# A two-layer graph attention kernel: every transfer of 125 rows issued as 112 rows and 13 rows

## The chip, the cores and the metric

The kernel runs on one core of one Trainium2 chip. The metric is the device time in microseconds of one execution. Before the change the median of three runs is 1033.21 us (1032.12 to 1034.33).

## The reference

Two graph attention layers over 1250 nodes and 20000 edges (plus a self loop for every node), then a residual sum and a layer norm. The first layer has 4 heads of 512 channels, the second one head of 768.

```python
def _gat_layer(x, src, dst, W, a_src, a_dst, bias, concat):
    h = (x @ W).reshape(N, H, C)
    al_s = jnp.einsum('nhc,hc->nh', h, a_src)
    al_d = jnp.einsum('nhc,hc->nh', h, a_dst)
    e = jax.nn.leaky_relu(al_s[src] + al_d[dst], 0.2)
    m = jax.ops.segment_max(e, dst, num_segments=N)
    ex = jnp.exp(e - m[dst])
    denom = jax.ops.segment_sum(ex, dst, num_segments=N)
    alpha = ex / (denom[dst] + 1e-16)
    out = jax.ops.segment_sum(h[src] * alpha[:, :, None], dst, num_segments=N)
    out = out.reshape(N, H * C) if concat else out.mean(axis=1)
    return out + bias

h = jax.nn.elu(_gat_layer(x, ..., W1, att_src1, att_dst1, b1, concat=True))   # 1250 x 2048
out = _gat_layer(h, ..., W2, att_src2, att_dst2, b2, concat=False)            # 1250 x 768
result = layernorm(x + out)
```

## The kernel before

The 1250 nodes are cut into 10 blocks of 125 (`B`), and 125 is the partition count of nearly every tile. The edges become a dense matrix of counts, `C[dst, src]`, and attention is done densely on it: per block of 125 destinations a row of 1250 scores, its exponential, times the counts, transposed on TensorE (line 476), and multiplied with the features `h`. Every product in float32 is made of three matmuls of split operands (lines 1243 to 1245, the helper `products`), so a block of a head costs 30 matmuls of 512 columns.

The stages in order of time:

- 0 to about 205 us: the edge lists become counts, x is loaded (`xall`, lines 486 to 489), transposed and stored (`xT_scratch`, L501), head 0's `h` is made.
- 205 to 684 us: four heads. Per block `j` of a head: TensorE makes the product, VectorE turns it into `vbuf` (L1099), ScalarE makes `ebuf` in two steps (L820, L822), VectorE finishes it (L1114), and SyncE stores 125 x 512 floats of `ebuf` into the DRAM scratch `hidden_scratch` (L535, `store_hid`). `ebuf` has two slots, so ScalarE at block j first waits until the store of block j-2 has landed (`hid_stored`, in `step` of the scalar program). Between two heads TensorE makes the next head's `h` from `xr` (L531, 128 rows), which is loaded back in blocks of 750 KB into three slots.
- 684 to about 872 us: the second layer's `h2`. Each block of 125 hidden rows of 2048 floats is loaded back (`hblk`, L545, `load_hb`, two slots), transposed on TensorE (L1353) and multiplied with `W2p`, which is 16 chunks `c` of 128 rows. Chunks 0 to 5 are loaded before the last head (`w2raw`) and split into high and low parts by ScalarE (L802) and GpSimd (L634) during its blocks 6 to 8. Chunks 6 to 15 (`w2late`, L538) are loaded after the last store of the last head; ScalarE (L802) and VectorE (L1129) split them.
- about 872 to 1030 us: second attention, with `xres` (L591) and `b2row` (L586) for residual and bias, and the store of `out` (L595) per block. The program ends when SyncE has seen all stores of `out` land.

All transfers are issued by SyncE, in program order, on one queue. What the order is at the turn from the heads to the second layer, in SyncE's program: at block 6 of the last head, the loads of `hblk` for blocks 0 and 1, then the stores of `ebuf` of blocks 6, 7, 8 and 9, then the ten loads of `w2late`, then two loads of `a2row`, then the other loads of `hblk`. An instruction that waits on SyncE holds all that stand behind it.

The transfers of 125 rows are: `b1row` (1000 KB, a broadcast), the 40 stores to `hidden_scratch` (250 KB each), the 10 loads of `hblk` (1000 KB each), two of `a2row` and one of `b2row` (375 KB, broadcasts), 10 loads of `xres` and 10 stores of `out` (375 KB each): 74 in all. The load of `xall` was already in two parts, rows 0 to 111 and rows 112 to 124 (`XP`). All others have 128 or 80 rows.

Of the kernel before, what the change touches and what calls it, by code (L numbers as in the profile page):

```python
# [26 lines left out]
B = 125  # L27
NB = N // B
PAIRS = E // (2 * B)
D = 768  # L30
# [33 lines left out]
WRING = 3  # L64
XL = 2
XP = 112
XW = 2
XR = 3

# [27 lines left out]
def gat_kernel(nc, x, src, dst, W1, as1, ad1, b1, W2, as2, ad2, b2, out):  # L97
# [4 lines left out]
    with ExitStack() as ctx:  # L102
# [378 lines left out]
        @block.sync  # L481
        def _(sp):
            sp.dma_start(dst_i[:], dst.rearrange("(p u e) -> p u e", u=2, e=B)).then_inc(ld_dst, 16)
            sp.dma_start(src_i[:], src.rearrange("(p u e) -> p u e", u=2, e=B)).then_inc(ld_src, 16)

            for i in range(NB // XL):
                for lo, hi in ((0, XP), (XP, B)):
                    sp.dma_start(xall[lo:hi, XL * i:XL * (i + 1), :], x[XL * i * B:XL * (i + 1) * B, :]
                                 .rearrange("(b p) d -> p b d", p=B)[lo:hi, :, :]).then_inc(ld_x[i], 16)

            def load_w1(h):
                sp.dma_start(w1raw[:], W1[:, h * HC:(h + 1) * HC].rearrange("(k p) c -> p k c", p=128)
                             ).then_inc(ld_w1, 16)

            sp.wait_ge(xt_ps, NB)
            load_w1(0)

            for j in range(NB):
                sp.wait_ge(xt_lo, j + 1)
                for u in range(2):  # L500
                    sp.dma_start(xT_d[j, :, u, :].rearrange("p (k n) -> p k n", k=KD), xa[:, u, :, j, :].bitcast(F32)).then_inc(xT_stored, 16)  # L501
            sp.wait_ge(ranges, 1)
            sp.dma_start(attr[:, 0:H, :], as1.rearrange("(o h) c -> o h c", o=1).broadcast_to([128, H, HC])
                         ).then_inc(ld_att, 16)
            sp.dma_start(attr[:, H:2 * H, :], ad1.rearrange("(o h) c -> o h c", o=1).broadcast_to([128, H, HC])
                         ).then_inc(ld_att, 16)

            sp.wait_ge(xT_stored, 32 * NB)  # L510
            sp.wait_ge(w1_hi, KD)
            sp.wait_ge(w1_lo, KD)
            for n in range(2 * KD):
                if n >= 3:
                    sp.wait_ge(wa_done, H * (n - 2))
                sp.dma_start(w1raw[:, 2 * (n % 3):2 * (n % 3) + 2, :],
                             W1[128 * (n // 2):128 * (n // 2) + 128, bass.ts(n % 2, 2 * HC)]
                             .rearrange("p (a c) -> p a c", a=2)).then_inc(ld_wk[n % 3], 16)
            sp.wait_ge(wa_done, 2 * H * KD)
            load_w1(1)  # L520


            sp.wait_ge(rows_ps, 3)
            sp.wait_ge(mm_done, NB)
            sp.dma_start(b1row[:], b1.rearrange("(o n) -> o n", o=1).broadcast_to([B, HID])).then_inc(ld_b1, 16)

            def load_xr(h, j):
                u = NB * (h - 1) + j
                if u >= XR:
                    sp.wait_ge(mm_done, 2 * NB * ((u - XR) // NB + 1) + (u - XR) % NB + 1)  # L530
                sp.dma_start(xr[:, u % XR, :, :].bitcast(F32), xT_d[j]).then_inc(ld_xr[u % XR], 16)  # L531

            def store_hid(h, j, s):
                sp.wait_ge(hid_done, NB * h + j + 1)
                sp.dma_start(hid_d[bass.ds(j * B, B), h * HC:(h + 1) * HC], ebuf[:, s, :]).then_inc(hid_stored[s], 16)  # L535

            def load_w2(c):
                sp.dma_start(w2_raw(c), W2[128 * c:128 * c + 128, :]).then_inc(ld_w2[c], 16)  # L538

            def load_hb(b, s):  # L540
                if isinstance(b, int) and b < 2:
                    sp.wait_ge(hid_stored[s], 8 * (H - 1) * NB + 16)
                else:
                    sp.wait_ge(ht_ps, 2 * b - 2)
                sp.dma_start(hblk[:, s, :], hid_d[bass.ds(b * B, B), :]).then_inc(ld_hb[s], 16)  # L545

            for h in range(H):
                if h == H - 1:
                    sp.wait_ge(mm_done, 2 * NB * (H - 1) + NB)
                    for c in range(WR):  # L550
                        load_w2(c)
                if h + 1 < H:
                    for j in range(XR):
                        load_xr(h + 1, j)

                def head(j, s):

                    if h == H - 1 and isinstance(j, int) and j == NB - 4:
                        load_hb(0, 0)
                        load_hb(1, 1)  # L560
                    store_hid(h, j, s)
                steps(sp, NB, 0, 4, head)
                if h + 1 < H:
                    for j in range(XR, NB):
                        load_xr(h + 1, j)
                if h + 2 < H:
                    sp.wait_ge(w1_hi, KD * (h + 2))
                    sp.wait_ge(w1_lo, KD * (h + 2))
                    load_w1(h + 2)


            sp.wait_ge(mm_done, 2 * H * NB)
            sp.wait_ge(v_done, H * NB)
            sp.wait_ge(w2_lo_p, WR)
            for c in range(WR, KC):
                if c >= KC - 2:
                    sp.wait_ge(hid_stored[c % 2], 16 * H * NB // 2)
                load_w2(c)
            sp.dma_start(a2row[:, 0, :], as2.broadcast_to([B, D])).then_inc(ld_a2, 16)
            sp.dma_start(a2row[:, 1, :], ad2.broadcast_to([B, D])).then_inc(ld_a2, 16)  # L580
            with sp.Fori(1, NB // 2) as k:
                for u in range(2):
                    load_hb(2 * k + u, u)

            sp.wait_ge(al2_done, 2 * NB)
            sp.dma_start(b2row[:], b2.rearrange("(o n) -> o n", o=1).broadcast_to([B, D])).then_inc(ld_b2, 16)  # L586

            def load_xres(b, s):
                if not (isinstance(b, int) and b < 2):
                    sp.wait_ge(y_b, b - 1)  # L590
                sp.dma_start(xres[:, s, :], x[bass.ds(b * B, B), :]).then_inc(ld_xres[s], 16)  # L591

            def store_out(b, s):
                sp.wait_ge(y_done, b + 1)
                sp.dma_start(out[bass.ds(b * B, B), :], y[:, bass.ds(b, 1), :].rearrange("p o n -> p (o n)")  # L595
                             ).then_inc(out_stored, 16)

            load_xres(0, 0)
            load_xres(1, 1)
            with sp.Fori(1, NB // 2) as k:  # L600
                for u in range(2):
                    load_xres(2 * k + u, u)
                    store_out(2 * k + u - 2, u)
            store_out(NB - 2, 0)
            store_out(NB - 1, 1)
            sp.wait_ge(out_stored, 16 * NB)


        @block.gpsimd
        def _(pool):  # L610
# [51 lines left out]
                pool_add(pool, H * NB + j, j % 2, prow2, arow2[:])  # L662

            def add_bias(b, s):
                pool.wait_ge(ld_xres[s], 8 * (b - s) + 16)
                pool.tensor_tensor(xres[:, s, :], xres[:, s, :], b2row[:], ALU.add).then_inc(xb_done, 1)

            pool.wait_ge(ld_b2, 16)
            add_bias(0, 0)

            def step2(j, s):
# [9 lines left out]
        def _(act):  # L681
# [122 lines left out]
            for h in range(H):  # L804
# [29 lines left out]
                        scores(nxt(4)[0], nxt(4)[1], s)  # L834

                def stored(h, j, s):
                    return 16 * (NB // 2) * h + 8 * (j - s)

                def split_w1_of(h1, k):
                    if isinstance(k, int) and k == 0:  # L840
# [19 lines left out]
            for c in range(W2E, KC):  # L860
                split_w2(c)
            for i in range(2):
                act.wait_ge(hid_stored[i], 16 * H * NB // 2)

            def h2_step(b, s):
                split_hT(2 * b + 2, b + 1, 0)
# [57 lines left out]
        def _(dve):  # L924
# [155 lines left out]
            dve_counts(dve, 2, 2, 0, prow)  # L1080
            dve_split(dve, 1, 1, PThi, PTlo)
            dve.wait_ge(bc_sb, H)
            dve.wait_ge(ld_b1, 16)

            def split_hT(n, half):
                dve.wait_ge(ht_hi, n + 1)
# [40 lines left out]
            for c in range(W2E, KC):  # L1127
                dve.wait_ge(w2_hi, c + 1)
                dve.tensor_tensor(W2p[:, c, 1, :], w2_raw(c), W2p[:, c, 0, :].bitcast(F32), ALU.subtract  # L1129
                                  ).then_inc(w2_lo, 1)  # L1130
            dve.wait_ge(ld_a2, 32)

            def scores2(b, s):

# [35 lines left out]
            maxima2(3)  # L1170
            dve_counts(dve, G2 + 2, 2, 0, prow2)
            dve_split(dve, G2 + 1, 1, PT2hi, PT2lo)
            dve.wait_ge(ld_b2, 16)

            def step2(j, s):
                g = G2 + j
# [14 lines left out]
                    dve_counts(dve, g + 3, j + 3, 1 - s, prow2)  # L1191
                if more(2):
                    dve_split(dve, g + 2, s, PT2hi, PT2lo)
                dve.wait_ge(ld_b2, 16)
                dve.wait_ge(y_b, j + 1)
                for a in range(2):
                    last = dve.bn_stats(bnst[:, a, :], y1[:, a * DH:(a + 1) * DH])
                last.then_inc(y_st, 1)
                dve.wait_ge(ld_b2, 16)
                dve.wait_ge(y_st, j + 1)  # L1200
                dve.bn_aggr(mv[:],
                            bnst[:].rearrange("p a n -> p (a n)")).then_inc(y_mv, 1)
# [11 lines left out]
        def _(pe):  # L1214
# [131 lines left out]

            def transpose_h(b, s, half):
                if half == 0:
                    pe.wait_ge(ld_hb[s], 8 * (b - s) + 16)
                if not (isinstance(b, int) and b == 0):  # L1350
                    pe.wait_ge(ht_lo, 2 * b + half - 1)
                for k in range(KH):
                    t = pe.transpose(PS[:, ht_banks(half)[k // 4], (k % 4) * B:(k % 4 + 1) * B],  # L1353
                                     hblk[:, s, (half * KH + k) * 128:(half * KH + k + 1) * 128], ident[0:B, 0:B])
                t.then_inc(ht_ps, 1)
# [124 lines left out]
```

## Time and profile before

| | |
|---|---|
| median of 3 runs | 1033.21 us |
| the profiled execution's own time | 1031.99 us |
| its span in the profile | 1030.2 us |
| TensorE (PE) busy | 913.7 us, 89% |
| VectorE (DVE) busy | 619.3 us, 60% |
| ScalarE (ACT) busy | 401.3 us, 39% |
| GpSimd (POOL) busy | 210.1 us, 20% |
| the 16 DMA engines, mean share | 29.1% |

The span is cut into 40 slices on the page. TensorE is at 9 tenths or more in nearly all slices from 220 to 870 us. Its dips after that are at about 875 to 900 us; a short one lies at 684 to 690 us, and the last 10 us have no matmul. "DMA share" in a window is the mean busy share of the core's 16 DMA engines, so one engine at work all the time counts 0.0625. In a timeline row the two numbers in front are the start and the duration in microseconds; for SPq rows that merge several issues, the duration reaches from the first to the end of the last. A bracket names how long the engine was idle before, and what it waited for.

### The profile page before, as it was taken

What the parts mean: (1) busy time and instruction counts of PE and PEld (TensorE: products, weight loads), DVE (VectorE), ACT (ScalarE), POOL (GpSimd) and SP (SyncE); (2) the same over time, 40 slices, a digit from 0 to 9 for tenths busy, and PEclk for the clock granted to TensorE, in tenths of its full rate; (3) what the DMA queues carried; (4) which work ended last, traced back from release to release, by engine and by line L of the source; (5) the groups of instructions that cost most, each with busy time, mean ns of one, the idle gap of its engine ahead of it and who ended that gap; (6) DMA issues with size and microseconds to landing.
All of it is one profiled execution on the core that took longest, in us unless ns stands there. A gap on an engine that the chain in (4) does not pass through costs nothing.

```text
span 1030.2 us, 13905 instructions
## 1 busy us (share of the span) xinstructions
PE 913.7 (89%) x4740; PEld 786.4 (76%) x4740; DVE 619.3 (60%) x1305; ACT 401.3 (39%) x574; POOL 210.1 (20%) x113
## 2 busy tenths in 40 slices
PE   0676788979999999999999999979999998479996
PEld 0454566668787788878887788869999998479995
DVE  9666568379987456863578645443221222988874
ACT  6454531256651366514663155542111112622220
POOL 1002000225530145202442023410000000343432
PEclk9987999989999999999999999989999999689998
DMA  6009975040115410263003431252111100101122
GB/s 155 1 7 191 150 227 171 7 128 27 32 32 191 179 31 29 66 219 126 30 30 102 138 103 37 93 191 111 58 63 40 74 6 1 44 21 57 59 64 69
DMA packets 38710, 86.65 MB, mean 84 GB/s; under 512 B 17251, under 2 KB 17411, under 8 KB 37032
## 3 DMA queue, kind: packets, MB, share of 16 engines
q1 hardware_dynamic: 38663, 86.04, 29.1%
q8 instruction: 28, 0.46, 0.2%
q14 instruction: 19, 0.16, 0.1%
HBM read 64.27 MB, written 21.76 MB: 84 GB/s over the span
## 4 chain that ended last, share of the span: by engine, by line
issue 38%; PE 27%; DVE 10%; ACT 8%; POOL 8%; SPq 4%; DMA 4%; DVEq 0%; POOLq 0%; ACTq 0%
PE ps L1243 7%; PE ps L1245 7%; PE ps L1244 7%; POOL prow L419 5%; SPq L501 4%; DVE junk_w L1032 2%; POOL W1lo L629 2%; PE ps L1353 2%; DMA hidden_scratch<-ebuf 2%; DMA xT_scratch<-xa 1%; PE ps L1274 1%; ACT prow L414 1%; DVE nbr L437 1%; DVE prow L456 1%; ACT oh_lo L701 1%
## 5 line engine op out<-in xcount | busy, mean ns | idle before, releaser
L419 POOL TENSOR_TENSOR prow<-prow,arow 125x1250 f32<-125x1250 f32 x50 | 139.3, 2789 | 633.4 <-ACT prow L414 633.4
L1243 PE MATMUL ps<-hhi,PThi 125*125 125x512 f32 x400 | 162.2, 405 | 1.0 <-DVE hlo L1019 1.0
L1244 PE MATMUL ps<-hlo,PThi 125*125 125x512 f32 x400 | 158.5, 396 | 0.0
L1245 PE MATMUL ps<-hhi,PTlo 125*125 125x512 f32 x400 | 158.1, 395 | 0.0
L425 ACT ACTIVATE prow<-prow,expb 125x1250 f32<-125x1250 f32 x50 | 67.0, 1340 | 172.7 <-POOL prow L419 151.5
L1243 PE MATMUL ps<-W2p,hT 128*125 128x384 f32 x320 | 110.6, 346 | 6.7 <-DVE W2p L1129 5.6
L1245 PE MATMUL ps<-W2p,hT 128*125 128x384 f32 x320 | 108.7, 340 | 0.0
L1244 PE MATMUL ps<-W2p,hT 128*125 128x384 f32 x320 | 108.5, 339 | 0.0
L1088 DVE TENSOR_TENSOR hT<-ps,hT 128x500 fp32r<-128x500 f32 x40 | 25.3, 674 | 128.4 <-ACT hT L797 124.0
L476 PE MATMUL ps<-ident,prow 125*125 125x125 f32 x500 | 68.1, 286 | 28.4 <-DVE prow L456 12.2
L476 PEld LDWEIGHTS ps<-ident,prow 125*125 125x125 f32 x500 | 65.0, 199 | 35.0 <-issue 30.6
L456 DVE SCALAR_TENSOR_TENSOR prow<-prow,counts 125x1250 f32<-125x1250 f32 x50 | 74.4, 1488 | 26.1 <-ACT prow L425 25.3
L1245 PEld LDWEIGHTS ps<-hhi,PTlo 125*125 125x125 f32 x400 | 74.6, 187 | 19.4
L1243 PEld LDWEIGHTS ps<-hhi,PThi 125*125 125x125 f32 x400 | 74.7, 187 | 18.6 <-DVE hlo L1019 1.5
L1244 PEld LDWEIGHTS ps<-hlo,PThi 125*125 125x125 f32 x400 | 74.6, 186 | 17.0
L441 DVE CUSTOM_DVE_ANT_0 nbr<-nbr,arow 125x1250 bf16<-125x1250 bf16 x50 | 77.3, 1546 | 2.1
L1046 DVE TENSOR_SCALAR ring<-table,ekey 125x420 bf16<-125x420 uint16 (+1 forms) x210 | 56.0, 341 | 34.5 <-issue 11.7
L694 ACT ACTIVATE hhi<-ps 125x512 fp32r<-125x512 f32 (+1 forms) x40 | 23.8, 597 | 134.9 <-PE ps L1245 134.9
L1243 PE MATMUL ps<-W1hi,xr 128*125 128x512 f32 x180 | 71.2, 396 | 2.1 <-DMA xr<-xT_scratch 2.1
L797 ACT ACTIVATE hT<-ps 128x500 fp32r<-128x500 f32 x40 | 21.3, 584 | 132.2 <-PE ps L1353 132.2
L1099 DVE SCALAR_TENSOR_TENSOR vbuf<-ps,rden,b1row 125x512 f32<-125x512 f32 x40 | 29.8, 746 | 69.1 <-PE ps L1245 69.1
L1244 PE MATMUL ps<-W1lo,xr 128*125 128x512 f32 x180 | 71.1, 395 | 0.0
(157 smaller groups left out, 1818.2 us busy)
## 6 DMA issues: line engine op xcount, KB each, us to landing
xr<-xT_scratch SPq DMA_DIRECT2D x30, 750.0 KB, 4.4
hidden_scratch<-ebuf SPq DMA_DIRECT2D x40, 250.0 KB
hblk<-hidden_scratch SPq DMA_DIRECT2D x10, 1000.0 KB
xT_scratch<-xa SPq DMA_DIRECT2D x20, 375.0 KB, 13.2
w1raw<-in_L_gnn_W SPq DMA_DIRECT2D x4, 1536.0 KB, 7.7
w1raw<-in_L_gnn_W SPq DMA_DIRECT2D x12, 512.0 KB, 3.6
w2late<-in_L_gnn_W SPq DMA_DIRECT2D x10, 384.0 KB, 8.0
xres<-in_x SPq DMA_DIRECT2D x10, 375.0 KB
```

The lines of the kernel that those rows point to most:

```text
L419: pool.tensor_tensor(buf[:, s, :], buf[:, s, :], row, ALU.add).then_inc(e_done, 1)
L425: act.activation(buf[:, s, :], buf[:, s, :], ACT.Exp, scale=SLOPE, bias=expb[:, bass.ds(g, 1)]).then_inc(p_done, 1)
L441: dve.tensor_tensor_reduce(out=scr[:], in0=scr[:], in1=row, scale=1.0, scalar=-3.0e38, op0=ALU.add, op1=ALU.max, accum_out=mx[:]).then_inc ...
L456: dve.scalar_tensor_tensor(buf[:, s, :], buf[:, s, :], 1.0, C[:, bass.ds(b, 1), :].rearrange("p o n -> p (o n)"), ALU.min, ALU.mult, accum ...
L476: t = pe.transpose(PS[0:B, 2 + bank, (b - lo) * B:(b - lo + 1) * B], buf[:, s, b * B:(b + 1) * B], ident[0:B, 0:B])
L501: sp.dma_start(xT_d[j, :, u, :].rearrange("p (k n) -> p k n", k=KD), xa[:, u, :, j, :].bitcast(F32)).then_inc(xT_stored, 16)
L1046: oh = dve.tensor_scalar(ring[:, w % 2, v, 0:win_cols(w)], table[:, w % TR, 0:win_cols(w)], ekey[:, bass.ds(at_slot(first, i, v), 1)], Non ...
L1088: lo = dve.tensor_tensor(ht_part(half, 1, a), PS[:, bank, 0:4 * B], ht_part(half, 0, a).bitcast(F32), ALU.subtract)
L1099: dve.scalar_tensor_tensor(vbuf[:, s, :], PS[0:B, s, :], rden[:, bass.ds(g, 1)], b1row[:, h * HC:(h + 1) * HC], ALU.mult, ALU.add).then_in ...
L1243: pe.matmul(dst, ahi, bhi, start=start, stop=False)
L1244: pe.matmul(dst, ahi, blo, start=False, stop=False)
L1245: return pe.matmul(dst, alo, bhi, start=False, stop=stop)
```

## The change

Each of the 74 transfers becomes two: rows 0 to 111 and rows 112 to 124 of the same tile, with the matching rows in DRAM. Both parts add 16 to the same semaphore, so every wait on one of these semaphores is doubled (`RS` is 32). Nothing else differs: buffers, engines, order and all other transfers are as before.

```diff
+RP = ((0, XP), (XP, B))
+RS = 16 * len(RP)
...
-            sp.dma_start(b1row[:], b1.rearrange("(o n) -> o n", o=1).broadcast_to([B, HID])).then_inc(ld_b1, 16)
+            for lo, hi in RP:
+                sp.dma_start(b1row[lo:hi, :], b1.rearrange("(o n) -> o n", o=1).broadcast_to([hi - lo, HID])).then_inc(ld_b1, 16)
...
             def store_hid(h, j, s):
                 sp.wait_ge(hid_done, NB * h + j + 1)
-                sp.dma_start(hid_d[bass.ds(j * B, B), h * HC:(h + 1) * HC], ebuf[:, s, :]).then_inc(hid_stored[s], 16)
+                for lo, hi in RP:
+                    sp.dma_start(hid_d[bass.ds(j * B + lo, hi - lo), h * HC:(h + 1) * HC], ebuf[lo:hi, s, :]).then_inc(hid_stored[s], 16)
...
                 if isinstance(b, int) and b < 2:
-                    sp.wait_ge(hid_stored[s], 8 * (H - 1) * NB + 16)
+                    sp.wait_ge(hid_stored[s], RS // 2 * (H - 1) * NB + RS)
                 else:
                     sp.wait_ge(ht_ps, 2 * b - 2)
-                sp.dma_start(hblk[:, s, :], hid_d[bass.ds(b * B, B), :]).then_inc(ld_hb[s], 16)
+                for lo, hi in RP:
+                    sp.dma_start(hblk[lo:hi, s, :], hid_d[bass.ds(b * B + lo, hi - lo), :]).then_inc(ld_hb[s], 16)
...
-            sp.dma_start(a2row[:, 0, :], as2.broadcast_to([B, D])).then_inc(ld_a2, 16)
-            sp.dma_start(a2row[:, 1, :], ad2.broadcast_to([B, D])).then_inc(ld_a2, 16)
+            for lo, hi in RP:
+                sp.dma_start(a2row[lo:hi, 0, :], as2.broadcast_to([hi - lo, D])).then_inc(ld_a2, 16)
+                sp.dma_start(a2row[lo:hi, 1, :], ad2.broadcast_to([hi - lo, D])).then_inc(ld_a2, 16)
...
             def store_out(b, s):
                 sp.wait_ge(y_done, b + 1)
-                sp.dma_start(out[bass.ds(b * B, B), :], y[:, bass.ds(b, 1), :].rearrange("p o n -> p (o n)")
-                             ).then_inc(out_stored, 16)
+                for lo, hi in RP:
+                    sp.dma_start(out[bass.ds(b * B + lo, hi - lo), :], y[lo:hi, bass.ds(b, 1), :].rearrange("p o n -> p (o n)")
+                                 ).then_inc(out_stored, 16)
...
-            sp.wait_ge(out_stored, 16 * NB)
+            sp.wait_ge(out_stored, RS * NB)
...
                 def stored(h, j, s):
-                    return 16 * (NB // 2) * h + 8 * (j - s)
+                    return RS * (NB // 2) * h + RS // 2 * (j - s)
```

`b2row` and `xres` are changed in the same way, and the waits for `ld_b1`, `ld_a2`, `ld_b2`, `ld_xres`, `ld_hb` and `hid_stored` on the other engines likewise. The programs of TensorE, VectorE, ScalarE and GpSimd keep every instruction and its place; only SyncE gets rows.

SyncE before, from the loads of `hblk` for blocks 0 and 1 in the last head to the first loop of the second layer:

```order
L545 DMA hblk<-hidden_scratch 125x2048 x2
L535 DMA hidden_scratch<-ebuf 125x512 x4
L538 DMA w2late<-in_L_gnn_W 128x768 x10
L579 DMA a2row<-in_L_gnn_att_src 125x768
L580 DMA a2row<-in_L_gnn_att_dst 125x768
```

SyncE now, at the same place:

```order
L550 DMA hblk<-hidden_scratch 112x2048
L550 DMA hblk<-hidden_scratch 13x2048
L550 DMA hblk<-hidden_scratch 112x2048
L550 DMA hblk<-hidden_scratch 13x2048
L539 DMA hidden_scratch<-ebuf 112x512
L539 DMA hidden_scratch<-ebuf 13x512
L539 DMA hidden_scratch<-ebuf 112x512
L539 DMA hidden_scratch<-ebuf 13x512
L539 DMA hidden_scratch<-ebuf 112x512
L539 DMA hidden_scratch<-ebuf 13x512
L539 DMA hidden_scratch<-ebuf 112x512
L539 DMA hidden_scratch<-ebuf 13x512
```

Behind these twelve the ten loads of `w2late` stand as before. Between the last product's store and the first load of `w2late` there is one more issue than before, and the load of `a2row` is now four issues.

SyncE before, at the end of a head and of the program (the last blocks' stores, and what follows them):

```order
L535 DMA hidden_scratch<-ebuf 125x512 x4
L531 DMA xr<-xT_scratch 128x1500 x7
L595 DMA out<-y 125x768 x2
```

SyncE now, the last block's store of a head with the loads of `xr` behind it, and the last two blocks of `out`:

```order
L539 DMA hidden_scratch<-ebuf 112x512
L539 DMA hidden_scratch<-ebuf 13x512
L534 DMA xr<-xT_scratch 128x1500 x7
L604 DMA out<-y 112x768
L604 DMA out<-y 13x768
L604 DMA out<-y 112x768
L604 DMA out<-y 13x768
```

One more issue stands ahead of the loads of `xr`, and one more behind the last product before the program can end.

## Rows read from the trace of the kernel before

**Rows 1.** The page: busy time by engine.

```profile
PE 913.7 (89%) x4740; PEld 786.4 (76%) x4740; DVE 619.3 (60%) x1305; ACT 401.3 (39%) x574; POOL 210.1 (20%) x113
```

**Rows 2.** Windows (start:end, length, busy by engine, PEclk, DMA share, GB/s): `hblk` and stores; `out`.

```profile
652.00:672.00 20.00, 20.00 (x102) 16.39 (x101) 7.90 (x13) 8.54 (x13) 7.76 (x4) 1.00 0.31 126
1025.00:1029.00 4.00, 0.00 (x0) 0.00 (x0) 0.00 (x0) 0.00 (x0) 0.00 (x0) 0.50 0.31 93
```

**Rows 3.** Windows: `w2late` of 128 rows; `xall` of 112 and 13 rows.

```profile
687.00:689.00 2.00, 0.00 (x0) 0.00 (x0) 0.23 (x1) 1.03 (x2) 0.00 (x0) 0.79 1.02 409
4.00:6.00 2.00, 1.21 (x5) 1.00 (x5) 1.79 (x9) 0.73 (x2) 0.00 (x0) 1.00 1.11 306
```

**Rows 4.** SyncE's timeline: the turn to the second layer, and `xall`.

```profile
649.77 0.71 SPq L545 DMA_DIRECT2D hblk<-hidden_scratch  x2
656.68 25.14 SPq L535 DMA_DIRECT2D hidden_scratch<-ebuf  x4
681.93 5.30 SPq L538 DMA_DIRECT2D w2late<-in_L_gnn_W  x10
689.46 2.11 SPq L545 DMA_DIRECT2D hblk<-hidden_scratch  x1
1.65 4.49 SPq L488 DMA_DIRECT2D xall<-in_x  x10
```

**Rows 5.** ScalarE's and VectorE's timeline at the same turn.

```profile
667.85 0.75 DVE L1099 SCALAR_TENSOR_TENSOR vbuf<-ps,rden,b1row 125x512 f32<-125x512 f32 x1 [3.49 <-PE ps L1245]
672.50 0.63 ACT L820 ACTIVATE ebuf<-vbuf 125x512 f32<-125x512 f32 x1 [7.63 <-DMA hidden_scratch<-ebuf]
678.73 0.74 DVE L1099 SCALAR_TENSOR_TENSOR vbuf<-ps,rden,b1row 125x512 f32<-125x512 f32 x1
680.84 0.69 DVE L1114 SCALAR_TENSOR_TENSOR ebuf<-ebuf,vbuf 125x512 f32<-125x512 f32 x1 [1.37 <-ACT ebuf L822]
687.90 9.33 ACT L802 ACTIVATE W2p<-w2late 128x768 fp32r<-128x768 f32 x10 [6.15 <-DMA w2late<-in_L_gnn_W]
688.77 9.45 DVE L1129 TENSOR_TENSOR W2p<-w2late,W2p 128x768 fp32r<-128x768 f32 x10 [5.73 <-ACT W2p L802]
```

**Rows 6.** TensorE's timeline at the same turn.

```profile
675.50 1.02 PE L1353 MATMUL ps<-ident,hblk 125*128 125x125 f32 x8
677.61 0.41 PE L1243 MATMUL ps<-W2p,hT 128*125 128x384 f32 x1 [1.09 <-issue]
683.82 0.34 PE L1245 MATMUL ps<-W2p,hT 128*125 128x384 f32 x1
689.79 0.68 PE L1243 MATMUL ps<-W2p,hT 128*125 128x384 f32 x1 [5.63 <-DVE W2p L1129]
695.16 0.42 PE L1243 MATMUL ps<-W2p,hT 128*125 128x384 f32 x1
```

**Rows 7.** Windows on TensorE's clock: two short gaps, and a long one.

```profile
208.00:210.00 2.00, 0.78 (x8) 0.59 (x6) 0.77 (x2) 2.00 (x4) 0.00 (x0) 1.00 1.03 250
210.00:212.00 2.00, 1.10 (x10) 1.10 (x11) 1.97 (x4) 2.00 (x4) 0.00 (x0) 1.00 1.03 234
691.00:693.00 2.00, 2.00 (x8) 2.00 (x7) 2.00 (x3) 1.77 (x3) 0.00 (x0) 0.50 1.03 415
```

**Rows 8.** Waits of TensorE, 204 to 700 us; its row in the first case; SyncE there.

```profile
PE ps L1243 <- DMA xr<-xT_scratch: 2.1, 3, 1.0
316.72 0.47 PE L1243 MATMUL ps<-W1hi,xr 128*125 128x512 f32 x1 [0.65 <-DMA xr<-xT_scratch]
309.84 6.58 SPq L531 DMA_DIRECT2D xr<-xT_scratch  x3
```

**Rows 9.** The page's DMA issues: KB each and us to landing.

```profile
xr<-xT_scratch SPq DMA_DIRECT2D x30, 750.0 KB, 4.4
```

**Rows 10.** The end: VectorE's last row, and SyncE's wait after its last issue.

```profile
1023.52 0.68 DVE L1207 TENSOR_SCALAR y<-y,mv,rstd 125x768 f32<-125x768 f32 x1 [0.66 <-POOL rstd L660]
SPq L102 <- DMA out<-y: 5.2, 1, 5.2
```

More of the change, by code:

```diff
@@ L576, in _ @@
                 if c >= KC - 2:
-                    sp.wait_ge(hid_stored[c % 2], 16 * H * NB // 2)
+                    sp.wait_ge(hid_stored[c % 2], RS * H * NB // 2)
                 load_w2(c)
-            sp.dma_start(a2row[:, 0, :], as2.broadcast_to([B, D])).then_inc(ld_a2, 16)
-            sp.dma_start(a2row[:, 1, :], ad2.broadcast_to([B, D])).then_inc(ld_a2, 16)
+            for lo, hi in RP:
+                sp.dma_start(a2row[lo:hi, 0, :], as2.broadcast_to([hi - lo, D])).then_inc(ld_a2, 16)
+                sp.dma_start(a2row[lo:hi, 1, :], ad2.broadcast_to([hi - lo, D])).then_inc(ld_a2, 16)
             with sp.Fori(1, NB // 2) as k:
@@ L585, in _ @@
             sp.wait_ge(al2_done, 2 * NB)
-            sp.dma_start(b2row[:], b2.rearrange("(o n) -> o n", o=1).broadcast_to([B, D])).then_inc(ld_b2, 16)
+            for lo, hi in RP:
+                sp.dma_start(b2row[lo:hi, :], b2.rearrange("(o n) -> o n", o=1).broadcast_to([hi - lo, D])).then_inc(ld_b2, 16)
             def load_xres(b, s):
@@ L590, in load_xres @@
                     sp.wait_ge(y_b, b - 1)
-                sp.dma_start(xres[:, s, :], x[bass.ds(b * B, B), :]).then_inc(ld_xres[s], 16)
+                for lo, hi in RP:
+                    sp.dma_start(xres[lo:hi, s, :], x[bass.ds(b * B + lo, hi - lo), :]).then_inc(ld_xres[s], 16)
             def store_out(b, s):
                 sp.wait_ge(y_done, b + 1)
-                sp.dma_start(out[bass.ds(b * B, B), :], y[:, bass.ds(b, 1), :].rearrange("p o n -> p (o n)")
-                             ).then_inc(out_stored, 16)
+                for lo, hi in RP:
+                    sp.dma_start(out[bass.ds(b * B + lo, hi - lo), :], y[lo:hi, bass.ds(b, 1), :].rearrange("p o n -> p (o n)")
+                                 ).then_inc(out_stored, 16)
             load_xres(0, 0)
@@ L664, in add_bias @@
             def add_bias(b, s):
-                pool.wait_ge(ld_xres[s], 8 * (b - s) + 16)
+                pool.wait_ge(ld_xres[s], RS // 2 * (b - s) + RS)
                 pool.tensor_tensor(xres[:, s, :], xres[:, s, :], b2row[:], ALU.add).then_inc(xb_done, 1)
-            pool.wait_ge(ld_b2, 16)
+            pool.wait_ge(ld_b2, RS)
             add_bias(0, 0)
@@ L862, in _ @@
             for i in range(2):
-                act.wait_ge(hid_stored[i], 16 * H * NB // 2)
+                act.wait_ge(hid_stored[i], RS * H * NB // 2)
             def h2_step(b, s):
@@ L1082, in _ @@
             dve.wait_ge(bc_sb, H)
-            dve.wait_ge(ld_b1, 16)
+            dve.wait_ge(ld_b1, RS)
             def split_hT(n, half):
@@ L1130, in _ @@
                                   ).then_inc(w2_lo, 1)
-            dve.wait_ge(ld_a2, 32)
+            dve.wait_ge(ld_a2, 2 * RS)
             def scores2(b, s):
@@ L1172, in _ @@
             dve_split(dve, G2 + 1, 1, PT2hi, PT2lo)
-            dve.wait_ge(ld_b2, 16)
+            dve.wait_ge(ld_b2, RS)
             def step2(j, s):
@@ L1193, in step2 @@
                     dve_split(dve, g + 2, s, PT2hi, PT2lo)
-                dve.wait_ge(ld_b2, 16)
+                dve.wait_ge(ld_b2, RS)
                 dve.wait_ge(y_b, j + 1)
@@ L1198, in step2 @@
                 last.then_inc(y_st, 1)
-                dve.wait_ge(ld_b2, 16)
+                dve.wait_ge(ld_b2, RS)
                 dve.wait_ge(y_st, j + 1)
@@ L1348, in transpose_h @@
                 if half == 0:
-                    pe.wait_ge(ld_hb[s], 8 * (b - s) + 16)
+                    pe.wait_ge(ld_hb[s], RS // 2 * (b - s) + RS)
                 if not (isinstance(b, int) and b == 0):
```

## The prediction

> **What bounds the kernel now.** I read the page's busy times first: TensorE works 89% of the span [rows 1], and from 220 to 870 us it hardly stops. A transfer can then cost time only where TensorE stands still and the chain behind it leads to the transfer. So I went on to the waits of each engine, then to the timelines around each wait that names a DMA, and last to windows over the DMA engines there. There are three such places.
>
> How fast a transfer goes. In the 20 us in which only `hblk` and stores of `ebuf` are under way, the mean share of the 16 DMA engines is 0.31, and 126 GB/s move; while `out` is stored it is 0.31 with 93 GB/s [rows 2]. 0.31 is 5 engines of 16. While `w2late` (128 rows) is loaded the share is 1.02 and 409 GB/s move, and while `xall` is loaded in parts of 112 and 13 rows it is 1.11 and 306 GB/s [rows 3] (a share of 1 is all 16; the records overlap a little). Per engine in use that is 25 GB/s for 125 rows and 26 GB/s for 128. So a transfer of 125 rows runs at a third of the speed only because it uses 5 engines. Each of those carries 25 rows. In two parts the fullest of 16 engines would carry 7 rows and 1 row, 8 in all: 0.32 of the time on the data. The Trainium skill, DMA: Bandwidth & Descriptors, "Why a DMA increments its semaphore by 16 and not by 1", says that a transfer is spread over the largest number up to 16 that divides its slowest dimension. By that rule 125 rows get 5, 112 get 16 and 13 get 13. With this the trace agrees, at 0.31 and about 1.
>
> **First place: the turn from the heads to the second layer.** What happens now:
> - 649.77: two loads of `hblk`, 1000 KB each, are issued, and at 656.68 the store of block 6 behind them [rows 4]. 2048 KB plus 256 KB (in thousands of bytes) at 126 GB/s are 18.3 us.
> - ScalarE reaches block 8 when its `vbuf` is done at 667.85 + 0.75 = 668.60, but needs the slot that the store of block 6 empties, and goes on at 672.50 [rows 5]: 3.9 us late (its 7.63 us of idle time began earlier, on VectorE).
> - VectorE waits for ScalarE's parts of block 8, so it takes the last product only at 678.73 though TensorE was done at about 675.7, where its next transposes start [rows 5, 6]. That is 3.0 us. From there to the end of `ebuf` it is 680.84 + 0.69 = 681.53, and the first `w2late` is issued at 681.93 [rows 4, 5].
> - Chunk 6 lands 5.9 us later; ScalarE begins to split it at 687.90, VectorE at 688.77, TensorE multiplies with it at 689.79. TensorE had run out of chunks at 683.82 + 0.34 = 684.16 and stood for 5.63 us. At the end of that gap its clock falls to 1.2 GHz (0.79 granted in 687 to 689, 0.50 in 691 to 693), and twelve matmuls and eight transposes go slowly until 695.16 [rows 3, 6, 7].
>
> What happens after: `hblk` and the store take 18.3 x 0.32 = 5.9 us of data and are done long before 668.6. ScalarE is not held. VectorE takes the last product at 675.7 instead of 678.73, and the store is issued at 681.56 - 3.0 = 678.55. One more issue stands behind it; ten of `xall`, large and small, took 4.49 us [rows 4], so I take 0.45 us, less than that by what an issue cost already; `w2late` is issued at 679.3. Its landing: an `xr` load of 750 KB lands 4.4 us after its issue [rows 9], of which 768 thousand bytes at 409 GB/s are 1.9 us, so 2.5 us are fixed. Chunk 6 is 393 thousand bytes, 1.0 us: landed at 679.3 + 3.5 = 682.8, plus 0.3 us for what is left of the last store, 683.1 (before, that store held 5 engines for 2 us at its front). Splitting takes the same 1.9 us (687.90 to 689.79), so TensorE can go on at 685.0. It starts `W2p` products at 676.7 rather than 677.61, as the 1.09 us wait [rows 6] is also ScalarE's and VectorE's delay, and runs out of chunks at 683.2. The gap is 1.8 us instead of 5.63. Two short gaps earlier (TensorE busy 0.78 us and 1.10 us of two successive 2 us windows) left the clock at 1.00 [rows 7], so I take 2.4 GHz after it. Twelve matmuls at 0.177 us (35 steps from 677.61 to 683.82) and the transposes at full speed take 3.0 us: 688.0 where before it was 695.16. VectorE splits a chunk in 0.95 us [rows 5] and TensorE uses one in six matmuls, 1.06 us, so no new wait follows. Gain 7.1 us. Bounds: 2.6 us if chunk 6 still takes 5.9 us to land and the clock falls too; 4.8 us if only the clock falls; 8.5 us if the gap closes altogether.
>
> **Second place: `xr` behind the last store of a head.** TensorE waits 2.1 us in all, three times, for an `xr` load [rows 8]. In the first case it is issued at 309.84 and TensorE goes on at 316.72, 6.9 us later, where 4.4 us is the median. The store just ahead holds 5 engines for 256/126 = 2.0 us, and each `xr` load needs all 16. In parts, the store holds them 0.65 us, and one issue of 0.45 us is added. Landing at 309.84 + 0.45 + 4.4 + 0.65 = 315.3, before TensorE's need at 316.07. Gain 2.0 us, between 0.5 and 2.1.
>
> **Third place: the last store.** VectorE ends at 1023.52 + 0.68 = 1024.20, and the program waits 5.2 us more after the last issue [rows 10], to the end of the span at 1030.2. The data runs from about 1025 to 1029 at 93 GB/s, 4.0 us [rows 2]. At 0.32 that is 1.3 us. The second part is issued 0.3 to 0.45 us after the first, but it has one row per engine and the first is still moving then. Gain 2.7 us; between 1.5 (the second issue and a landing of its own are added in full) and 2.9.
>
> **What is hidden.** Elsewhere loads of `hblk` come two blocks ahead of TensorE: 1024/126 = 8.1 us of data where ten blocks take some 188 us (684 to 872). `a2row`, queued behind the ten loads of `w2late`, comes late for VectorE, but TensorE is at work all that time, so its earlier landing gains nothing. `b1row`, `b2row` and `xres` land ahead of use. The 74 extra issues cost SyncE some 0.3 to 0.45 us each; it waits on others most of the time, and beside the places above nothing is queued behind them within a microsecond.
>
> **Sum.** 7.1 + 2.0 + 2.7 = 11.8 us. From the profiled execution's own 1031.99 us that gives 1020.2. The median of the three runs is 1.2 us higher, so by it 1021.4. I say 1021.
>
> **Rivals.**
> - The turn gains less: chunk 6 lands late, or TensorE's clock falls in the new gap after all. Speaks for it: the gap is an estimate within a chain of five instructions, and SyncE may be held up (one issue took 2.11 us at 689.46 [rows 4]). Against: the two short gaps [rows 7]. 2.6 to 4.8 us in place of 7.1: 1023.6 to 1026.
> - The parts bring nothing: the share of 0.31 would be set by something other than the row count, or the two parts run one behind the other for as long as the whole. No term of the sum is left: 1033. Against it stands `xall`, at 306 GB/s in such parts [rows 3]. The Trainium skill, DMA: Bandwidth & Descriptors, "Rules for kernel authors", advises against two transfers to disjoint partition halves, since both spread over all 16 engines and serialize. By that rule alone the change would be worth nothing; it supposes halves that already use all 16, which 0.31 does not show.
> - Slower: SyncE's issues. If an issue blocks whenever an earlier one is still in progress, as perhaps in the one of 2.11 us, each second part takes not 0.45 but 4 us. Then the three `xr` loads land at 309.84 + 4.0 + 4.4 = 318.2 instead of 316.6, 1.6 us worse each, 4.9 in all; `w2late` is issued at 683.0 and gains only 1.4; the end is 0.2 us later. Sum 3.7 us slower: 1036. At 2.1 us an issue it would still gain some 5 us, so it decides from about 3.3 us an issue on. Against: `xall`'s 0.45 us, with nine transfers outstanding.
>
> **How the numbers follow.** A difference within 0.2% (about 2 us) can't be told from none. Forecast, 1021, with its own range 1018.5 to 1023.5: 0.68. Less gain at the turn: 0.18. Nothing: 0.08. Slower by the issues: 0.06. Faster takes the first two and a little of the others, 0.88; same 0.06; slower 0.06. The range 1017.5 to 1027.5 holds the first two and leaves out the others.
>
> **What would show it.** Right: the DMA share near 1 while `hblk` is loaded, ScalarE's wait for a store gone, `w2late` issued about 4 us after TensorE's last product instead of 6, TensorE's gap before chunk 6 about 2 us with the clock at 1.00, no wait of TensorE for `xr`, and some 2.5 to 3 us from the last issue to the end. Wrong: a share that stays at 0.31, issues of the parts of 13 rows of over 2 us, or a new wait of TensorE after chunk 6.

## The result, and the profile after

| | before | in two parts |
|---|---|---|
| median | 1034.34 us (6 runs, 1032.12 to 1035.71) | 1025.09 us (6 runs, 1021.14 to 1026.52) |
| ratio | | 0.9906, 95% interval 0.9884 to 0.9927 |
| the profiled execution's own time | 1031.99 us | 1021.14 us |
| its span | 1030.2 us | 1019.0 us |
| last row of VectorE to the end of the span | 6.0 us | 3.1 us |

The kernel is 9.3 us faster by the medians. 11.8 us were forecast, and 1021 us. The median lies 4 us above that: outside 1018.5 to 1023.5, which the prediction gave to its main forecast, inside the wider range of 1017.5 to 1027.5, and in the part of it that belongs to the first rival (1023.6 to 1026). That the profiled execution took 1021.14 us, just what was forecast, is luck: it was the fastest of six.

The DMA engines, as windows of the trace after (columns as in [rows 2]): the loads of `hblk`, and the last store of `out`.

```profile
648.00:656.00 8.00, 8.00 (x41) 6.57 (x41) 4.55 (x8) 5.20 (x7) 3.33 (x2) 1.00 0.99 250
1016.80:1018.00 1.20, 0.00 (x0) 0.00 (x0) 0.00 (x0) 0.00 (x0) 0.00 (x0) 0.50 0.92 282
```

The share is 0.99 and 0.92 where it was 0.31 in both places. The rate has doubled for `hblk` (126 to 250 GB/s) and tripled for `out` (93 to 282).

The turn to the second layer: SyncE, then ScalarE, VectorE and TensorE in the trace after, to be read against [rows 4 to 6].

```profile
646.92 1.60 SPq L550 DMA_DIRECT2D hblk<-hidden_scratch  x4
653.24 22.58 SPq L539 DMA_DIRECT2D hidden_scratch<-ebuf  x8
675.96 5.73 SPq L542 DMA_DIRECT2D w2late<-in_L_gnn_W  x10
665.17 0.63 ACT L829 ACTIVATE ebuf<-vbuf 125x512 f32<-125x512 f32 x1 [3.76 <-DVE vbuf L1108]
680.20 2.65 ACT L811 ACTIVATE W2p<-w2late 128x768 fp32r<-128x768 f32 x3 [4.94 <-DMA w2late<-in_L_gnn_W]
664.38 0.75 DVE L1108 SCALAR_TENSOR_TENSOR vbuf<-ps,rden,b1row 125x512 f32<-125x512 f32 x1 [3.48 <-PE ps L1254]
672.22 0.75 DVE L1108 SCALAR_TENSOR_TENSOR vbuf<-ps,rden,b1row 125x512 f32<-125x512 f32 x1 [0.70 <-PE ps L1254]
679.02 0.34 PE L1254 MATMUL ps<-W2p,hT 128*125 128x384 f32 x1
682.09 0.44 PE L1252 MATMUL ps<-W2p,hT 128*125 128x384 f32 x1 [2.73 <-DVE W2p L1138]
686.41 0.66 PE L1252 MATMUL ps<-W2p,hT 128*125 128x384 f32 x1
```

ScalarE starts block 8 at once after `vbuf` (665.17), no longer held by a DMA. `w2late` is issued 10.8 us after that `vbuf` is done (13.3 before). TensorE still stands before chunk 6, for 2.73 us instead of 5.63.

The window just behind that gap:

```profile
684.00:686.00 2.00, 2.00 (x10) 1.90 (x9) 1.73 (x2) 1.62 (x2) 0.00 (x0) 0.50 1.04 418
```

The granted clock is 0.50 there, the level of 1.2 GHz (1.00 is 2.4 GHz): it fell after a gap of 2.7 us. At the end, SyncE's waits (in total, times, longest) have 1.9 us where it was 5.2 [rows 10], and VectorE's last row stands 3.1 us ahead of the end of the span:

```profile
SPq L104 <- DMA out<-y: 1.9, 1, 1.9
```

```profile
1015.23 0.68 DVE L1216 TENSOR_SCALAR y<-y,mv,rstd 125x768 f32<-125x768 f32 x1 [0.66 <-POOL rstd L669]
```

TensorE waits for `xr` nowhere in this profile (2.1 us before [rows 8]).

**Where the time went.** Five stretches of a profile, each between two rows of VectorE or ScalarE, give a ledger. "Start" ends with the first `vbuf` of the program (229.4 before, 228.2 after). "Heads" goes from there to the start of `vbuf` of block 8 of the last head (667.85, 664.38). "Turn" goes on to the first `h2f` of the second layer. "Rest" ends with VectorE's last row, "end" with the span. The last column is the clock granted in a window behind TensorE's gap before chunk 6. The row that ends the turn, from ScalarE's timeline before and, in the second fence, after:

```profile
705.72 0.82 ACT L855 ACTIVATE h2f<-ps 125x768 f32<-125x768 f32 x1
```

```profile
697.24 0.82 ACT L864 ACTIVATE h2f<-ps 125x768 f32<-125x768 f32 x1
```

| us | start | heads | turn | rest | end | clock after the gap |
|---|---|---|---|---|---|---|
| before | 229.4 | 438.5 | 37.9 | 318.5 | 6.0 | 0.50 |
| in two parts | 228.2 | 436.2 | 32.9 | 318.7 | 3.1 | 0.50 |
| only `out` | 236.4 | 438.8 | 38.2 | 318.6 | 3.1 | 0.50 |
| only stores to `hidden_scratch` | 234.8 | 436.9 | 33.5 | 318.7 | 5.9 | 0.50 |
| only `hblk` | 234.6 | 438.8 | 35.1 | 319.1 | 5.9 | 0.50 |
| only the other four | 234.7 | 438.8 | 38.3 | 318.7 | 5.9 | 0.50 |
| 124 and 1 | 234.9 | 444.5 | 43.9 | 320.7 | 8.3 | 0.50 |
| 100 and 25 | 233.8 | 436.9 | 31.4 | 319.9 | 4.8 | 1.00 |
| in two parts, again | 237.0 | 436.3 | 33.1 | 318.5 | 3.1 | 0.52 |
| in two parts, a third time | 234.0 | 436.5 | 31.4 | 318.2 | 3.1 | 1.00 |
| with filler matmuls | 234.1 | 436.5 | 31.1 | 318.4 | 3.1 | 1.00 |

Heads, turn and end change by -2.3, -5.0 and -2.9 us, 10.2 in all. The other 1 us of the two profiles' difference is the start, 1.2 us shorter, less 0.2 in the rest. It can't be put down to the change. `b1row` is the only transfer of the start that the change cuts, and cutting it does not shorten the start: 234.7 us in "only the other four", where it is cut, against 234.6 to 236.4 in the three experiments beside it, where it is whole. Among the profiles of the changed kernel alone the start varies more than any other stretch (228.2, 237.0, 234.0). The experiments ran later, on three chips, and there the kernel before took 1038 to 1039 us, so only ratios and stretches are compared.

### The profile page after: what moved, and what is told of

Read it like the earlier page. It is cut to its first block, busy times and chain, and to the rows that moved or that the text cites. A ratio compares the mean times of both kernels' runs of the same rounds, so it can differ in the third digit from the quotient of the medians.

```text
span 1019.0 us, 14075 instructions
## 1 busy us (share of the span) xinstructions
PE 912.0 (89%) x4740; PEld 785.3 (77%) x4740; DVE 619.4 (61%) x1305; ACT 401.4 (39%) x574; POOL 210.3 (21%) x113
## 4 chain that ended last, share of the span: by engine, by line
PE 66%; DVE 13%; issue 8%; SPq 4%; ACT 4%; DMA 3%; POOL 1%; DVEq 1%; POOLq 0%; ACTq 0%
PE ps L1252 19%; PE ps L1254 19%; PE ps L1253 19%; SPq L503 4%; PE ps L478 4%; DVE junk_w L1041 2%; DVE prow L458 2%; PE ps L1362 2%; DVE nbr L439 1%; DMA xT_scratch<-xa 1%; PE ps L1283 1%; ACT oh_lo L710 1%; DVE mneg L446 1%; DVE negm L448 1%; POOL xres L675 1%
## 5 line engine op out<-in xcount | busy, mean ns | idle before, releaser
L1108 DVE SCALAR_TENSOR_TENSOR vbuf<-ps,rden,b1row 125x512 f32<-125x512 f32 x40 | 29.8, 746 | 69.5 <-PE ps L1254 69.4
## 6 DMA issues: line engine op xcount, KB each, us to landing
xT_scratch<-xa SPq DMA_DIRECT2D x20, 375.0 KB, 13.3
```

Source lines behind the costliest of these rows:

```text
L1108: dve.scalar_tensor_tensor(vbuf[:, s, :], PS[0:B, s, :], rden[:, bass.ds(g, 1)], b1row[:, h * HC:(h + 1) * HC], ALU.mult, ALU.add).then_in ...
```

## The experiments

**Only `out`, only the stores, only `hblk`, only the rest.** In each, the tensors named are in two parts and all others whole. Here it is for the store of `out`, the only tensor cut in the first kernel, against the changed kernel; the names behind # are the places where the line stands:

```diff
+R1 = ((0, B),)
-                for lo, hi in RP:      # store_hid, load_hb, load_xres, a2row, b1row, b2row
+                for lo, hi in R1:
```

> Only the stores of out are in two parts. Theory (a transfer of 125 rows uses 5 of 16 engines, 112 use 16): the time from VectorE's last row to the end falls from 6.0 us to about 3.1, as with the whole change; nothing else moves; 2.9 us faster in all. Rival (each part costs its own landing, one after the other): no gain at the end or a loss of up to 2 us. ScalarE's wait for a store and TensorE's three waits for xr stay.

Measured: 1035.5 us against 1037.99, ratio 0.9974 (0.9961 to 0.9987), 2.5 us by the medians; the end takes 3.1 us where it took 6.0; heads, turn and rest are as before within 0.3 us. The gain at the end is shown, and it is that of the whole change.

> Only the 40 stores to hidden_scratch are in two parts. Theory: TensorE's three waits for xr (2.1 us) go. At the turn to the second layer hblk still holds 5 engines until about 671 us, so the share of the store that falls on these lands only behind it: ScalarE's late start falls from 3.9 to about 2.5 us, and w2late's first chunk lands sooner since no store of 2 us stands in front of it. 4 to 5 us faster in all. Rival (the loads of hblk do all of it): under 1 us.

Measured: ratio 0.9946 (0.9929 to 0.9963), 5.8 us faster. Of TensorE's three waits for `xr` one is left, of 0.6 us, and the heads take 436.9 us where the kernels with whole stores take 438.8. ScalarE's idle time before block 8 falls from 7.6 to 5.1 us, by 2.5 us where 1.4 were expected. `w2late`'s first chunk lands sooner, as these rows of SyncE's and ScalarE's timeline show:

```profile
683.77 5.70 SPq L543 DMA_DIRECT2D w2late<-in_L_gnn_W  x10
688.20 1.71 ACT L812 ACTIVATE W2p<-w2late 128x768 fp32r<-128x768 f32 x2 [5.10 <-DMA w2late<-in_L_gnn_W]
```

4.4 us from issue to use, where it was 6.0 [rows 4, 5].

> Only the ten loads of hblk are in two parts. Theory: ScalarE's wait for the store at block 8 goes, w2late is issued 3 us earlier, but its first chunk still takes nearly 6 us to land behind a store on 5 engines, so TensorE's gap before chunk 6 is about 3.5 us and its clock falls. TensorE's three waits for xr stay, the end stays at 6.0 us. 3 to 3.5 us faster in all. Together with the stores alone it should make up what the whole change gives less the 2.9 us of the end. Rival (stores do all): under 1 us.

Measured: ratio 0.9986 (0.9972 to 1.0), 1.3 us by the medians, less than the 3 to 3.5 us expected and hardly told from none. The mechanism is in the profile: ScalarE's wait is gone, `w2late` is issued at 684.46 and used at 690.43, still 6.0 us later; TensorE stands 3.93 us, and the clock falls. The turn is 2.8 us shorter than in the first profile, 3.1 than in the two beside it that leave the turn alone; the rest is 0.4 us longer than there, for no cause that was found.

> Only b1row, a2row, b2row and the ten loads of xres are in two parts. Theory: these were hidden, so no difference within 2 us, and the profile shows the same waits as before, but for VectorE's wait for a2row, which gets shorter by some 2 us with no gain. Rival (one of them stood on the path): over 2 us faster.

Measured: ratio 1.0002 (0.9986 to 1.0019). Heads, turn, rest and end are those of the kernel with only `out` cut and of the kernel before, within 0.4 us but for the end. VectorE's wait for `a2row`, 4.3 us before, is gone and gains nothing. That `b1row`, `a2row`, `b2row` and `xres` were hidden is shown, to within the interval's 2 us.

The stores and `hblk` alone shorten the turn by 4.4 and 2.8 us, together by 5.0. Both shorten the same wait of ScalarE, which can go only once: the stores take 2.5 us of it, `hblk` takes all 3.9. The quicker landing of chunk 6 (1.5 us) comes with the stores alone.

**Other cuts.** The parts are rows 0 to 123 and row 124:

```diff
-RP = ((0, XP), (XP, B))
+RP = ((0, 124), (124, B))
```

> Every transfer of 125 rows in two parts, rows 0 to 123 and row 124. Theory (the number of engines is the largest divisor of the row count up to 16: 4 and 1): the fullest engine carries 32 rows instead of 25, the DMA share while hblk is loaded is 0.25, the store of block 6 lands about 5 us later, so the turn is 5 to 7 us longer, the end 1 to 1.5 us, the waits for xr 1 to 3 us more: 7 to 11 us slower than the kernel before. Rival (two parts as such, in flight at once, make the gain): as fast as with 112 and 13. Rival (only the issues count): 0 to 2 us slower.

Measured: 1055.68 us against 1038.1, ratio 1.0178 (1.0154 to 1.0202), 17.6 us slower. Direction and mechanism are as the theory of engine counts has it; the size was put too low, at 7 to 11 us. A window of its trace while `hblk` is loaded:

```profile
672.00:680.00 8.00, 8.00 (x43) 6.54 (x41) 2.81 (x5) 3.90 (x6) 3.72 (x2) 1.00 0.25 104
```

A share of 0.25 is 4 engines of 16. ScalarE's idle time before block 8 is 12.9 us, the turn 6.0 us longer, the end 2.3, the rest 2.2, and the heads 6.1 (5.7 against the profiles beside it). TensorE's waits while it makes the next head's `h` are 7.1 us (2.1 put down to `xr`, 5.0 to VectorE's `hlo`), 3.1 before (2.1 and 1.0). ScalarE's wait, and one of TensorE's that the profile puts down to `hlo`:

```profile
689.29 0.63 ACT L829 ACTIVATE ebuf<-vbuf 125x512 f32<-125x512 f32 x1 [12.91 <-DMA hidden_scratch<-ebuf]
574.98 0.46 PE L1252 MATMUL ps<-W1hi,xr 128*125 128x512 f32 x1 [2.39 <-DVE hlo L1028]
```

By the times of issue and by the program, that wait and its like at 449.01 (1.67 us) are for `xr`. The first `xr` load behind the last store of the head is issued at 315.95, 441.27 and 567.03, and TensorE goes on at 323.90, 449.01 and 574.98, 7.95, 7.74 and 7.95 us later (6.9 in each head before). The program asks there only for the `hlo` of the product before the one just made, and that was done some 4 us earlier. So TensorE stood 6.1 us for `xr` where it stood 2.1. The store ahead of these loads was in two parts here too. Two parts as such bring nothing.

Then rows 0 to 99 and 100 to 124:

> Every transfer of 125 rows in two parts, rows 0 to 99 and 100 to 124. Theory: 10 engines and 5, of which the first 5 carry 15 rows, 0.6 of the time of 25 rows. The store of block 6 lands before ScalarE needs it, the waits for xr nearly go, the end is 1.3 to 1.8 us shorter. 6 to 8.5 us faster than before, so 1 to 3 us slower than 112 and 13. Rival (any split into two gives the same): equal to 112 and 13, with 3.1 us from VectorE's last row to the end.

Measured: 1032.85 us against 1038.1, ratio 0.9954 (0.9936 to 0.9973), while 112 and 13 on the same chip gave 0.9908 (0.9883 to 0.9932). The window over the loads of `hblk`:

```profile
654.00:664.00 10.00, 10.00 (x55) 8.38 (x55) 5.31 (x9) 5.53 (x8) 4.20 (x3) 1.00 0.61 156
```

0.61 is 10 engines. By the medians this kernel is 5.3 us faster than before and 4.8 us slower than 112 and 13: a point between the two, as the theory has it, but less gain than the 6 to 8.5 us expected (the interval reaches from 2.8 to 6.6). The end is 4.8 us, 1.2 shorter. The profiled execution, at 1028.62 us, was 4.2 us faster than the median. In it the clock held after a gap of 2.67 us, so that the turn took 31.4 us; the profiles of the changed kernel put that at 1.6 us, and what else made the other runs slower is not known.

**The changed kernel again.**

> The changed kernel once more, word for word, to see how far its times and TensorE's granted clock vary. Its runs so far lie between 1021.1 and 1026.5 us at a mean clock of 0.966 to 0.961. Expected: a median of 1023 to 1027, and, where a profile has the lower clock, more slow matmuls behind the gap before chunk 6 or at another gap; if all slow matmuls lie elsewhere, the spread has nothing to do with the change.

Measured: 1028.08 us against 1038.1, ratio 0.9908 (0.9883 to 0.9932), the same as in the first comparison. Its six runs lie from 1026.0 to 1030.2, the 17 of the kernel before beside it from 1034.6 to 1040.2: the scatter is there without the change. 1023 to 1027 us were expected, from the first chip's times. The gap is 2.96 us and the clock falls.

> The changed kernel a third time, beside the one with chunks 6 and 7 of w2late early, on the same chip. Expected 0.9% faster than before (0.9885 to 0.993); the stretch from block 8's vbuf to the first h2f 32.9 to 33.1 us, unless the clock holds through the gap, then 31.1.

Measured: 1027.34 us against 1039.09, ratio 0.9888 (0.9871 to 0.9904). Here the clock held after a gap of 2.85 us, by a window and by TensorE's timeline:

```profile
688.00:690.00 2.00, 1.69 (x10) 1.70 (x11) 1.89 (x3) 1.77 (x3) 0.00 (x0) 1.00 1.03 410
```

```profile
688.31 0.44 PE L1252 MATMUL ps<-W2p,hT 128*125 128x384 f32 x1 [2.85 <-DVE W2p L1138]
```

The turn is 31.4 us, 6.5 less than before. TensorE waited 0.3 us for one `xr` load. So in one of three profiles of the same program the clock stays up, and it is worth 1.6 us (33.0 less 31.4).

**What the clock costs: matmuls in the gap.**

```diff
                     if isinstance(b, int) and b == 0:
+                        if c == W2E:
+                            pe.wait_ge(v_done, H * NB)
+                            for n in range(14):
+                                pe.matmul(PS[0:B, n % 2, 0:DH], hT[:, 0, 0, 0, :], W2p[:, 0, 0, 0:DH], start=True, stop=True)
                         w2_lo_done(pe, c)
```

> The changed kernel with 14 extra matmuls of 384 columns on TensorE, into accumulators nobody reads, between chunk 5 and chunk 6 of block 0 of the second layer: they fill about 2.5 of the 2.7 to 3.0 us in which it waits for w2late. Theory (the term for the turn was too large because TensorE's clock fell after that gap all the same): the clock stays at 1.00 through 680 to 700 us and the stretch from block 8's vbuf to the first h2f is 1.3 to 1.7 us shorter than in the changed kernel (31.2 to 31.7 us instead of 32.9 and 33.1); the total is 1 to 2 us faster than the changed kernel. Rival (the missing 2 us lie in the landing of chunk 6 alone): the stretch stays at 32.9 us.

Measured: the clock is 1.00 from 680 to 700 us, and the turn takes 31.1 us, within what was expected. The windows behind chunk 6:

```profile
686.00:690.00 4.00, 3.89 (x22) 3.57 (x21) 2.83 (x4) 3.39 (x4) 0.00 (x0) 1.00 1.03 400
690.00:694.00 4.00, 4.00 (x28) 3.96 (x27) 4.00 (x5) 3.58 (x5) 0.00 (x0) 1.00 1.03 414
```

The drop of the clock costs 1.8 to 2.0 us (32.9 and 33.1 less 31.1). In the run times this is not to be told from the changed kernel: ratio 0.9901 (0.9884 to 0.9918).

**Loading `w2late` ahead of the last store.**

```diff
+                    if h == H - 1 and isinstance(j, int) and j == NB - 1:
+                        sp.wait_ge(w2_lo_p, WR)
+                        for c in range(WR, WR + 5):
+                            load_w2(c)
                     store_hid(h, j, s)
...
-            for c in range(WR, KC):
+            for c in range(WR + 5, KC):
```

> The changed kernel, and SyncE issues the loads of chunks 6 to 10 of w2late ahead of the last store of the last head, as soon as the first six chunks are split. Theory: chunk 6 then lands at about 676 us instead of 680, before TensorE has used up chunk 5 at 679.4; the gap of 2.7 us and the slow clock behind it go: 4 us faster than the changed kernel, 13 to 14 us faster than before. Rival (TensorE's gap comes from the splitting on ScalarE and VectorE, not from the landing): under 1 us against the changed kernel.

Measured: 1026.68 us against 1038.1, ratio 0.9895 (0.9872 to 0.9918), where the changed kernel had 0.9908 (0.9883 to 0.9932): no difference that can be told. 4 us were expected. TensorE no longer waits for chunk 6, but stands 1.36 us for chunk 8. That load was the third of the five, issued at 681.12 (the issue alone took 1.50 us), and it was used at 689.55, 8.4 us later; the clock holds, and the turn takes 30.6 us.

> As the kernel with five chunks of w2late ahead of the last store, but with chunks 6 and 7 only. There chunk 8 landed 8 us after its issue, and TensorE stood 1.4 us for it. Theory (the landing gets longer with what is in flight around it, so that issuing more early gains nothing for chunk 8): chunk 8 lands no later than there although it is issued 3 us later, TensorE's gaps sum to 1.5 us or less, total within 1 us of the one with five. Rival (the order on SyncE decides): chunk 8 is 3 us later and the gap grows to 4 us.

Measured: with two chunks early (`WR + 2` in both places) 1026.22 us against 1038.39, ratio 0.9881 (0.9865 to 0.9896). As the theory had it, chunk 8 is issued 2.8 us later, at 683.91, and used at 689.08: 16.8 us after block 8's `vbuf` begins, where it was 17.3 with five early. That what is in flight sets the landing fits this, but it is argued: no run changed that alone.

```profile
683.91 5.00 SPq L542 DMA_DIRECT2D w2late<-in_L_gnn_W  x8
689.08 1.75 ACT L815 ACTIVATE W2p<-w2late 128x768 fp32r<-128x768 f32 x2 [2.90 <-DMA w2late<-in_L_gnn_W]
691.06 0.41 PE L1256 MATMUL ps<-W2p,hT 128*125 128x384 f32 x1 [0.81 <-DVE W2p L1142]
```

TensorE's gaps are 0.81 and 0.84 us, the clock holds, and the turn takes 29.3 us.

> Chunks 6 and 7 of w2late ahead of the last store, once more, for a direct comparison with the changed kernel. By the profile of its first run the stretch at the turn is 3.7 us shorter (29.3 us), so 2.5 to 4 us faster than the changed kernel in total and 1.2% faster than before. Rival (its first profile was a lucky one, and the gain is the clock's alone): 1.9 us or less.

Measured, on one chip with the third run of the changed kernel: 1026.18 us and 1027.34 us, ratios 0.9882 (0.9865 to 0.9899) and 0.9888 (0.9871 to 0.9904). 2.5 to 4 us between them were expected. The turn takes 29.8 us against 31.4 us, both with the clock held. The shorter turn is in both profiles of this kernel, but 1.2 us by the medians is within the intervals: that this kernel beats the changed one is not shown by its times. The rival, 1.9 us or less, is nearer.

## Why the prediction was right, and where it was off

**The five engines.** Shown. 125 rows give a share of 0.31, 112 and 13 give 0.99, 124 and 1 give 0.25, 100 and 25 give 0.61; and the time follows, from 0.9906 to 1.0178. By the rule of the Trainium skill, DMA: Bandwidth & Descriptors, "Why a DMA increments its semaphore by 16 and not by 1", the whole transfer gets 5 engines and the large parts 16, 4 and 10, and the shares agree; what the small parts (13, 1, 25 rows) get, no share here tells. The advice of the Trainium skill, DMA: Bandwidth & Descriptors, "Rules for kernel authors", against two transfers to disjoint partition halves does not hold where the whole one gets 5 engines: by it alone the ratio would be 1.

**The end**: 2.7 us forecast, 2.9 measured. **`xr`**: 2.0 forecast; the waits are gone in two of three profiles, 0.3 us is left in the third, and the heads are 2.3 us shorter.

**The turn**: 7.1 us forecast, 5.0 and 4.8 measured in two profiles and 6.5 in a third. This is the term that was mis-sized, and of the steps in it one: "so I take 2.4 GHz after it". In two of three profiles the clock fell all the same, and that costs 1.6 to 1.9 us (against the third profile, and against the filler kernel, whose turn is 6.8 us shorter than before). The other 0.3 to 0.6 us are the longer gap. It was put at 1.8 us and was 2.7 to 3.0, and the two short gaps of [rows 7] say nothing of gaps that long. The reason for the longer gap is the landing of chunk 6, 4.2 to 4.5 us after its issue instead of 3.8, and TensorE's earlier end with chunk 5. The other steps fit: ScalarE not held; the issue of `w2late` 10.8 us after `vbuf` of block 8, forecast 10.7; 1.9 us from ScalarE's split to TensorE. The first rival, less gain at the turn because the clock falls (4.8 us), is what happened in these two profiles. So the mechanism of all three places was right, and one term too large; the stated range took in the rival too, and the median needed that.

Two side sums of the turn do not come out, and neither enters the forecast: with the gap closed altogether the gain would be 7.1 + 1.8 = 8.9 us, not 8.5; and with `w2late` issued at 683.0, 3.7 us later than forecast, 4.8 - 3.7 = 1.1 us would be left by the slower clock, not 1.4.

**A step that was wrong and cost nothing**: `hblk` was to take 0.32 of its time, as the rows per engine do. It took half: each of 16 engines moved only 16 GB/s against 25 of each of 5. That one rate per engine does not hold was to be seen in [rows 2], where `out` at the same share moves 93 GB/s, 19 per engine. The load needed only to be done well before ScalarE's block 8 at 665 us, and at 250 GB/s it takes 8.2 us from about 648.

**The issues**: a second part cost SyncE about 0.4 us (two stores in 0.8 us, four loads of `hblk` in 1.60), and none of the 120 issues of parts of the stores, of `hblk` and of `out` took over 0.41 us. The rival with 4 us an issue did not occur. The other rival, parts that bring nothing, falls with the first line of this section.

The forecast of a difference, 11.8 us, compares with 10.2 in the ledger and with 9.3 by the medians of the first comparison. On two other chips the medians differ by 10.0 and 11.8 us. So the times alone do not refute 11.8; it is the turn in the profiles that shows the term to be too large. Of the 4 us between 1021 and the median, 1.1 come from the starting point: the forecast went from the median of three runs, 1033.2, and that of six is 1034.3.

## What to carry to other kernels

Look at the DMA share in a window in which one kind of transfer is alone: a share of 0.31 at 126 GB/s says that the transfer is spread over 5 engines, and the row count is what to change (here by cutting off the largest multiple of 16 rows); the count of parts is not, as 124 and 1 showed. Such a cut is worth only what waits behind the transfer, 10 us here of 74 transfers, three places in all. Where a gap of TensorE shrinks but stays at 2.7 to 3.0 us, give the sum with either clock behind it, and price the lower one from a stretch at that level.

## What the runs showed of the hardware that was not expected

- The rate of an engine depends on what is loaded. Loading `hblk` from `hidden_scratch`, 5 engines moved 126 GB/s (25 each), 10 moved 156 and 16 moved 250 (16 each), while `w2late` on 16 engines moved 409 to 418. `out` shows no such drop: 93 GB/s on 5 engines and 282 on 16, 18 to 19 each. Two parts as such are not the cause, since 124 and 1 moved 104 GB/s on 4 engines (26 each). Why an engine moves less of `hblk` where 10 or 16 are at work was not tried.
- TensorE's clock after gaps of nearly one length: it fell after 2.73 and 2.96 us, and held after 2.67 and 2.85 us.
- How long a load of 384 KB takes to land hangs on what is around it. In the changed kernel the first of ten, right behind the last store, was in use 4.2 to 4.5 us after its issue, and the third 5.2 us after (676.84 to 682.01). The third of five issued ahead of that store was in use only 8.4 us after. The cause is open.
